# Values spread by DMAs, layer 3's heads on their own array rows, and probabilities turned in two row halves

## The chip, the cores and the metric

One core of a Trainium2 chip runs the whole program. The metric is the device time of that core in microseconds, from the first to the last instruction and what lies around them; less is better. TensorE is PE in the profile (PEld is its weight load), VectorE is DVE, ScalarE is ACT, GpSimd is POOL, SyncE is SP. A "q" behind the name means the engine's sequencer, which waits, counts and issues DMAs.

## The reference

Four Swin blocks follow one another on x of shape (16, 56, 56, 96), float32. Each one normalizes, shifts the image by 3, cuts it into windows of 7x7 = 49 tokens, attends inside each window with a learned bias and a mask, projects, adds, normalizes again and runs an MLP of 96, 384 and 96 channels. Layers 0 to 2 have 12 heads of 8 channels, layer 3 has 4 heads of 24.

```python
qkv = (xw @ qkv_w + qkv_b).reshape(B*nW, N, 3, NH, hd)
q, k, v = qkv[:, :, 0], qkv[:, :, 1], qkv[:, :, 2]
attn = einsum('wqhd,wkhd->whqk', q * hd**-0.5, k) + rel_bias
attn = softmax(attn + attn_mask)
o = einsum('whqk,wkhd->wqhd', attn, v).reshape(B*nW, N, C)
x = x + roll(window_reverse(o @ proj_w + proj_b))
m = gelu(ln(x) @ fc1_w + fc1_b)      # layer 3 normalizes m again here
x = x + (m @ fc2_w + fc2_b)
```

## The kernel before

The batch is cut into 4 groups of 4 images. A group's tokens (128 pairs of windows) stay in `x`, which has room for two groups, while all four layers run over them. A pair of windows has 98 tokens on 98 partitions (two windows of N = 49). Four pairs are a quad, so a stage, attention or MLP of one layer, has NQ = 32 quads. `quad_steps` (L232) calls a body for each quad: four quads in straight code, the rest two at a time in a loop, and two more at each end, where `on(d)` says whether quad i+d exists. Every engine runs the same schedule; the order on each engine is the order in which its body is written, and semaphores (`a_...`) join them. `wait(s, u)` (L260, its waits show as L262) stands until quad or pair u is counted on s. The order on each engine is strict: what stands behind a wait waits too.

The body of attention has four slots, s = 0 to 3, one for each pair of quad i. A pair goes through this chain:

- PE, L697: scores of pair s. Layers 0 to 2: three groups of 4 heads, each on 32 rows of the array (`QT` and `Kbd`, keys spread block-diagonally over a head slot and zeros), each into its own bank (0 to 2); layer 3: one group on all 96 rows. Windows 0 and 1 of the pair land on output partitions 0 to 48 and 64 to 112.
- DVE, L992 and L994: the bias is added while the scores are read from PSUM, then the maximum of each head is taken. POOL, L465, subtracts it. ACT, L555, takes the exponential in place, in `S`.
- PE, L753, in the next slot: one transpose per pair of heads turns 113 x 98 probabilities into 98 x 113 in PSUM (6 for 12 heads, 2 for 4 heads; banks 3 and 4). ACT, L579, copies them to `PT`.
- PE, L711, two slots later: `PT` times values, 2 per pair of heads, into bank 5 (`Ops`), with a column of ones that gives the sum. Both heads of a pair are contracted at once, so `Vbd` holds the values block-diagonally, with zeros where key and head don't match.

Around that, once per quad, PE also runs: in slot 0 the output projection of quad i-2 (L719, `Yps`, bank 6) and the first half of the values of quad i+1 (L675, 4 matmuls, bank 7); in slot 1 keys (L667, bank 6) and queries (bank 7) of quad i+1; in slot 2 the other half of the values (4 matmuls); in slot 3 the transposes of the outputs `Ot` (L738) and of the normalized tokens of quad i+2 (L745). For the values the tokens of each window stand twice in `hT`, so that the product has them on all 98 partitions, and DVE (L966) multiplies by the 0/1 mask `vmask` on the way into `Vbd`, twice a quad. DVE also adds the residual (L999, slot 0), takes statistics (L838 and L846, slot 1), and in slot 2 divides by the sums: `rec` at L1006, `Ot` at L1010. Since `Ops` is one bank, PE's product for the first pair of the next quad, which stands in slot 3, waits for `Ot`:

```python
if s == 3:
    wait(a_o, i - 1)
    wait(a_v0e, i)
```

ACT copies the keys four times, each with another `kmask` column (`key_slot`, L535), and the queries once (L560), all in slots 1 and 2. An fp32 matmul shows as two instructions in the profile, a transpose as one.

SP loads the constants (L343 to L371), then layer 0's mask, two DMAs a quad of 49 x 4 runs of 196 bytes (`mask_quad`, L302), each in turn when its place is free; and a group's tokens in 228 DMAs in and 228 out (`tokens`, L287). Stores of group g-1 and then loads of group g+1 are issued from the end of layer 0's attention of group g.

Of the kernel before, what the change touches and what calls it, by code (L numbers as in the profile page):

```python
# [30 lines left out]
TABLE = 2 * WS - 1  # L31
P = 128
# [48 lines left out]
def constants():  # L81
# [5 lines left out]
    c["kmask"] = np.stack([((ch // 8) % 4)[:, None] == np.arange(4)[None],  # L87
                           (ch // 24)[:, None] == np.arange(4)[None]], 1).astype(np.float32).reshape(C, 8)

    half = (np.arange(2 * N) // N)[:, None]  # L90
    c["vmask"] = np.concatenate([(half == (np.arange(w) // (w // 2))[None]) for w in (16, 48)],
                                1).astype(np.float32)
    c["vones"] = (half == np.arange(2)[None]).astype(np.float32)
# [16 lines left out]
def build(nc, d, x_in, out):  # L110
    ctx = ExitStack()
    with ctx:
# [3 lines left out]
        def sem(name):  # L116
# [17 lines left out]
        kmask = sb("kmask", [C, 2, 4])  # L134
        vmask = sb("vmask", [2 * N, 64])
        vones = sb("vones", [2 * N, 2])
        average = sb("average", [PAIR, PAIR])
        wqkv = sb("wqkv", [C + 1, LAYERS, 3 * C])
# [9 lines left out]
        hT = sb("hT", [C + 1, QUAD, 2, 2, N])  # L148
        QT = sb("QT", [C, 2, QUAD, PAIR])
# [3 lines left out]
        PT = sb("PT", [PAIR, 4, 6, 2, N])  # L153
        Vroom = sb("Vroom", [PAIR, 2 * QUAD * 2 * 108])
# [15 lines left out]
        Vbd = Vroom[:, :].rearrange("p (s j w t n) -> p s j w t n", s=2, j=QUAD, w=2, t=6)  # L170
        Vbd3 = Vroom[:, 0:2 * QUAD * 2 * 100].rearrange("p (s j w t n) -> p s j w t n", s=2, j=QUAD, w=2, t=2)
# [14 lines left out]
        a_xn, a_t1, a_ht, a_v0, a_v0e, a_k, a_ke, a_q, a_qe, a_v2, a_v2e = (sem(n) for n in (  # L186
            "xn_ready", "xnT_done", "hT_ready", "v_first_done", "v_first_ready", "k_done", "k_ready",
            "q_done", "q_ready", "v_second_done", "v_second_ready"))
# [6 lines left out]
        s_ones = sem("output_pads_set")  # L195
        s_stand = sem("waits_held")
# [23 lines left out]
        PTps = ps[0:PAIR, 3:5, 0:3 * P].rearrange("p b (g q) -> p b g q", q=ROW2)  # L220
        O_BANK, Z_BANK, X_BANK = 5, 6, 7
        XTps = ps[0:C, X_BANK, 0:QUAD * PAIR]
        Vps = ps[0:PAIR, X_BANK, 0:4 * C]
        Kps = ps[0:C, Z_BANK, 0:QUAD * PAIR]
# [7 lines left out]
        def quad_steps(eng, base, body, full=4):  # L232
# [13 lines left out]
            for i in range(NQ - skew, NQ + skew + 1):  # L246
                body(Unit(0, base, i, 0, pbase), i, lambda d: 0 <= i + d < NQ)

# [60 lines left out]
        def mask_stream(sp, g):  # L309
            with sp.Fori(2, NQ, 2) as q:  # L310
                for j in range(2):
                    sp.wait_ge(a_mb, g * NP + q * QUAD + (j - 1) * QUAD)
                    mask_quad(sp, g, q + j, j)

# [22 lines left out]
        def _(sp):  # L337
# [7 lines left out]
            load(kmask[:, :, :].rearrange("p a b -> p (a b)"), d["kmask"])  # L345
            load(vmask[:, :], d["vmask"])
            load(vones[:, :], d["vones"])
            load(average[:, :], d["average"])
            for l in range(LAYERS):
# [7 lines left out]
                load(wqkv[0:C, l, :], d[k["wqkv"]])  # L357
                load(wqkv[C:C + 1, l, :], row("bqkv"))
# [15 lines left out]
            mask_stream(sp, 0)  # L374
            with sp.Fori(1, GROUPS) as g:

                tokens(sp, g, False, s_x)
                sp.wait_ge(a_mb, g * NP)
                for q in range(2):
                    mask_quad(sp, g, q, q)  # L380
                sp.wait_ge(s_x, (g + 1) * (16 * LOADS))
                sp.sem_inc(s_next, 1)
                sp.wait_ge(s_fin, g)
                stand(sp)
                mask_stream(sp, g)
                tokens(sp, g - 1, True, s_out)
                sp.wait_ge(s_out, g * (16 * TOK_DMAS))
                stand(sp)
# [12 lines left out]
        def _(pool):  # L401

            for t in (mask0, room):
                pool.memset(t[:], 0.0)
# [710 lines left out]
```

## Time and profile before

| | |
|---|---|
| Time, median of 3 runs | 9466.97 us (9449.72 to 9478.86) |
| Time of the profiled execution | 9446.19 us |
| Its span | 9444.4 us |
| Mean granted TensorE clock | 0.970 |
| PE busy | 8794.8 us (93%), 110128 matmuls |
| PEld busy | 6584.9 us (70%) |
| DVE busy | 6697.5 us (71%) |
| ACT busy | 5517.5 us (58%) |
| POOL busy | 5081.6 us (54%) |

The first and last start of a score matmul (L697) bound each attention stage. For the second group they are 2503.9 and 2882.6 in layer 0, 3081.8 and 3473.0 in layer 1, 3662.0 and 4053.0 in layer 2, 4242.8 and 4516.5 in layer 3; between them lie the MLPs. A matmul's length includes its way through the array, and matmuls overlap, so the time that one costs is the step from one start to the next, not its length.

### The profile page before, as it was taken

Reading aid. Unit: us, or ns where it says so; the run is one execution under the profiler, and the core shown is the slowest. Engines: PE = TensorE matmul, PEld = TensorE weight load, DVE = VectorE, ACT = ScalarE, POOL = GpSimd, SP = SyncE. Lnnn points to the kernel's source line nnn. Section 1 sums busy time; section 2 is a strip of 40 time slices with the busy share of each in tenths; the row PEclk is TensorE's granted clock in tenths of the full one; section 3 lists DMA queues with packets and bytes.
Section 4 is the critical chain, followed back from the end, with each engine's and each line's share of the span. In section 5 each row is a group of like instructions: output and inputs, shape, how many; then the busy total and the mean of one; then the engine's idle time right before and its main releaser. Section 6 shows DMA issues by size and latency. Waiting matters only on the chain.

```text
span 9444.4 us, 315493 instructions
## 1 busy us (share of the span) xinstructions
PE 8794.8 (93%) x110128; PEld 6584.9 (70%) x110128; DVE 6697.5 (71%) x19998; ACT 5517.5 (58%) x9632; POOL 5081.6 (54%) x6190
## 2 busy tenths in 40 slices
PE   2999999998999999999899999999989999999986
PEld 1777777776677777777567677777657777777764
DVE  3777767667776676767877677776686767677676
ACT  1756647465574665746567375664656657465554
POOL 5865646553484554645258465554527756455441
PEclk8999999999999999999999999999999999999998
DMA  2010000000001000000000100000000000000000
GB/s 35 7 22 3 0 1 0 1 1 0 4 6 30 15 1 1 0 1 0 0 5 9 33 8 1 1 0 1 0 0 7 19 8 0 1 1 1 1 0 21
DMA packets 177967, 57.28 MB, mean 6 GB/s; under 512 B 176379, under 2 KB 177412, under 8 KB 177499
## 3 DMA queue, kind: packets, MB, share of 16 engines
q1 hardware_dynamic: 158592, 47.28, 2.7%
q10 hardware_dynamic: 14027, 3.47, 0.2%
q8 instruction: 242, 3.96, 0.2%
q0 software_dynamic: 4880, 0.71, 0.1%
q14 instruction: 226, 1.85, 0.1%
HBM read 31.71 MB, written 19.27 MB: 5 GB/s over the span
## 4 chain that ended last, share of the span: by engine, by line
PE 41%; issue 25%; POOL 13%; DVE 12%; DVEq 3%; POOLq 2%; ACT 1%; ACTq 1%; DMA 0%
PE ps L711 5%; PE ps L753 5%; PE ps L697 5%; PE ps L667 4%; PE ps L675 4%; PE ps L768 4%; PE ps L791 4%; POOL G L451 4%; POOL S L465 3%; PE ps L719 3%; DVE xn L945 3%; DVE bst L838 2%; DVE bst L1055 2%; POOL rstd L439 2%; PE ps L738 2%
## 5 line engine op out<-in xcount | busy, mean ns | idle before, releaser
L465 POOL TENSOR_TENSOR S<-S,mx 113x588 f32<-113x588 f32 (+1 forms) x2048 | 2062.3, 1007 | 1995.2 <-DVE mx L994 1973.4
L579 ACT ACTIVATE PT<-ps 98x588 f32<-98x588 f32 (+1 forms) x2048 | 1178.5, 575 | 998.4 <-PE ps L753 955.3
L992 DVE TENSOR_TENSOR S<-ps,bias 113x588 f32<-113x588 f32 (+1 forms) x1536 | 970.4, 632 | 921.6 <-PE ps L697 907.7
L711 PEld LDWEIGHTS ps<-Vroom,PT 98*49 98x49 f32 x40960 | 1174.8, 128 | 543.7 <-issue 513.2
L535 ACT ACTIVATE room<-ps,kmask 96x392 f32<-96x392 f32 x2048 | 1190.1, 583 | 447.7 <-PE ps L667 447.7
L994 DVE TENSOR_REDUCE mx<-S 113x12 f32<-113x588 f32 (+1 forms) x2048 | 1359.3, 664 | 70.4
L753 PE MATMUL ps<-ident,S 113*98 113x113 f32 x10240 | 1366.2, 265 | 23.2 <-ACT S L555 23.0
L711 PE MATMUL ps<-Vroom,PT 98*49 98x18 f32 (+1 forms) x40960 | 1330.8, 202 | 34.6 <-DVE Ot L1010 12.0
L555 ACT ACTIVATE S<-S 113x588 f32<-113x588 f32 (+1 forms) x2048 | 1239.2, 605 | 64.0 <-POOL S L465 62.3
L768 PEld LDWEIGHTS ps<-w,G 128*98 128x98 f32 x12288 | 1144.4, 168 | 112.8 <-issue 61.1
L753 PEld LDWEIGHTS ps<-ident,S 113*98 113x98 f32 x10240 | 1055.0, 129 | 233.1 <-issue 192.5
L697 PE MATMUL ps<-room,QT 32*64 32x196 f32 (+2 forms) x20480 | 1162.2, 350 | 1.5 <-issue 0.2
L768 PE MATMUL ps<-w,G 128*98 128x96 f32 x12288 | 1155.0, 251 | 0.0
L838 DVE BATCH_NORM_STATS2 bst<-x 98x6 f32 (+1 forms) x4224 | 880.9, 254 | 237.3 <-DMA G<-k_mask_dram 119.3
L675 PE MATMUL ps<-wqkv,hT 97*98 97x96 f32 x8192 | 925.1, 256 | 0.7 <-ACT hT L571 0.6
L503 POOL TENSOR_TENSOR x<-x,c 98x384 f32 x512 | 512.1, 1000 | 714.9 <-DVE xn L945 714.9
L439 POOL TENSOR_TENSOR rstd<-rstd,neghalf 98x4 f32 (+1 forms) x768 | 786.9, 1025 | 144.7 <-POOL rstd L436 144.7
L791 PE MATMUL ps<-h,w 97*128 97x392 f32 x2304 | 833.3, 498 | 13.4 <-ACT G L604 10.8
L675 PEld LDWEIGHTS ps<-wqkv,hT 97*98 97x98 f32 x8192 | 798.8, 168 | 45.0 <-issue 12.7
L667 PE MATMUL ps<-hT,wqkv 97*96 97x392 f32 x2048 | 815.1, 519 | 0.0
L604 ACT ACTIVATE G<-ps 128x1176 f32<-128x1176 f32 x384 | 441.7, 1150 | 534.2 <-PE ps L791 534.1
L451 POOL TENSOR_TENSOR G<-bias,mask 113x588 f32<-113x588 f32 x512 | 683.4, 1335 | 0.0
(80 smaller groups left out, 11710.3 us busy)
## 6 DMA issues: line engine op xcount, KB each, us to landing
mask<-L_conv_mask_matrix_dram SPq DMA_DIRECT2D x256, 37.5 KB
x<-x_dram SPq DMA_DIRECT2D x56, 84.0 KB
out_dram<-x SPq DMA_DIRECT2D x48, 84.0 KB
x<-x_dram SPq DMA_DIRECT2D x234, 10.5 KB
out_dram<-x SPq DMA_DIRECT2D x228, 10.5 KB
out_dram<-x SPq DMA_DIRECT2D x180, 18.4 KB
x<-x_dram SPq DMA_DIRECT2D x168, 18.4 KB
x<-x_dram SPq DMA_DIRECT2D x64, 48.0 KB
```

What stands on the lines that cost most here:

```text
L465: pool.tensor_tensor(v, v, m, ALU.subtract).then_inc(a_sub, 1)
L535: return act.activation(Kbd[:, o, :, :, a, :].rearrange("p j w n -> p (j w) n"), Kps.rearrange("p (g n) -> p g n", n=N), ACT.Copy, scale=k ...
L555: act.activation(S[:, e, 0:nh * N], S[:, e, 0:nh * N], ACT.Exp).then_inc(a_exp, 1)
L579: act.activation(PT[:, (s + 3) % 4, 0:blocks, :, :].rearrange("p (b t) w n -> p b (t w) n", b=banks), PTps[:, 0:banks, 0:2 * k, 0:N], ACT. ...
L667: return pe.matmul(dst.rearrange("p (g n) -> p g n", n=N), wqkv[:, l, col:col + C], at, start=True, stop=True)
L675: last = pe.matmul(Vps[:, at:at + C], twice, wqkv[:, l, 2 * C:3 * C], start=True, stop=True)
L697: last = pe.matmul(out, q, Kbd[rows, t, s, w, :, :].rearrange("p a n -> p (a n)"), start=True, stop=True)
L711: last = pe.matmul(Ops[ROW2 * w:ROW2 * w + N, p, b, :], PT[:, p, b, w, :], room_of[:, o if s < 3 else t, p, w, b, :], start=True, stop=True)
L753: last = pe.transpose(at.rearrange("p w q -> p (w q)")[:, 0:TOK], S[:, e, PAIR * b:PAIR * (b + 1)], ident[0:TOK, 0:TOK])
L768: last = pe.matmul(ps[0:PAIR, 6 + t, C * j:C * (j + 1)], G[:, t, c, PAIR * j:PAIR * (j + 1)], w2[:, l, c, :], start=(c == 0), stop=(c == H ...
L791: last = pe.matmul(ps[:, 2 + c, 0:QUAD * PAIR], w1[:, l, P * c:P * (c + 1)], h4[:, s, :, :].rearrange("p a q -> p (a q)"), start=True, sto ...
L994: dve.reduce_max(mx[:, e, 0:nh], S[:, e, 0:n].rearrange("p (h k) -> p h k", k=N), axis=AX.X).then_inc(a_mx, 1)
```

## The change

Four things change.

1. Values. The four matmuls per quad (L675 becomes one block in slot 2) take each pair's 98 tokens once; `hT` holds them once. The columns of the value weights are loaded in an order that puts even heads first, then odd heads. DVE copies the product once per quad into `Vd`, where each head is followed by a column that holds 1. Then SP issues four DMAs per quad, each of 49 partitions x 4 pairs x 54 floats (50 in layer 3), which put `Vd` into the block-diagonal `Vbd`, whose zeros are set once at the start. SP waits for the copy (`a_vd`) and for the products of the quad that used this half of `Vbd`; PE waits for the landing (`s_vb`) before the first product of a quad, behind its wait for `Ot`, and DVE waits for the landing of the previous quad before it overwrites `Vd`.
2. SP's program becomes the same `quad_steps` as the engines'. Mask loads stand behind the spread in each body of layer 0. A group's stores follow the attention of layer 0, the next group's loads that of layer 1.
3. Layer 3. Query and key weights are loaded with each head's 24 columns in a group of 32 (the rest zero), so each head has 32 rows of the array. Scores are 8 matmuls of 49 columns instead of 2 of 196, into banks 0 to 3; ACT copies the keys once (128 x 392, `Kfull`) instead of four times.
4. Turning. With 12 heads, each window's rows of `S` are turned apart: 12 transposes of 49 rows, window 0 into bank 3 and window 1 into bank 4, instead of 6 of 113 rows. Layer 3 keeps its two.

Orders change with it: the key projection moves from slot 1 to 0 (bank 7), the queries stay in slot 1 (bank 6), ACT's first key copy now stands ahead of the exponential in slot 1, its last one in slot 3, and the copy into `hT` behind that into `PT`. On PE a count on `s_stand` stands between the waits and the transposes.

```diff
-        Vroom = sb("Vroom", [PAIR, 2 * QUAD * 2 * 108])
+        Vd = sb("Vd", [PAIR, QUAD, 2, HALF])
+        Vbd = sb("Vbd", [PAIR, 2, QUAD, 2, 2, HALF])
...
+                    def spread(i, j, on):
+                        if on(1):
+                            wait(a_vd, i + 1)
+                            stand(sp)
+                            wait(a_pv, i - 1)
+                            stand(sp)
+                            par = (j + 1) % 2
+                            for w in range(2):
+                                for a in range(2):
+                                    sp.dma_start(Vbd[N * a:N * (a + 1), par, :, w, a, 0:width],
+                                                 Vd[N * w:N * (w + 1), :, a, 0:width]).then_inc(s_vb[par], 16)
...
+                    quad_steps(sp, base, spread, 4)
+                    if l == 0 and g > 0:
+                        sp.wait_ge(s_fin, g)
+                        tokens(sp, g - 1, True, s_out)
+                    if l == 1 and g + 1 < GROUPS:
+                        if g > 0:
+                            sp.wait_ge(s_out, g * (16 * TOK_DMAS))
+                        tokens(sp, g + 1, False, s_x)
...
+                            if s == 1 and on(1):
+                                wait(a_k, i + 1)
+                                if nh == 12:
+                                    key_slot(0)
+                                else:
+                                    act.activation(Kfull[:, o, :, :].rearrange("p j n -> p (j n)"), Kps,
+                                                   ACT.Copy).then_inc(a_ke, 1)
+                            if s == 3 and nh == 12 and on(1):
+                                key_slot(3).then_inc(a_ke, 1)
...
-                                for k in range(3 if nh == 12 else 1):
-                                    rows = slice(32 * k, 32 * (k + 1)) if nh == 12 else slice(0, C)
+                                for k in range(3 if nh == 12 else 4):
+                                    rows = slice(GRP * k, GRP * (k + 1))
...
                                 if s == 3:
                                     wait(a_o, i - 1)
-                                    wait(a_v0e, i)
-                                if s == 1:
-                                    wait(a_v2e, i - 1)
+                                    spread = (g * LAYER_QUADS + l * NQ + i.index - t + 2) * 32
+                                    pe.wait_ge(s_vb[t], spread if i.static else pe.snap(spread))
...
                             if s == 0 and on(1):
                                 wait(a_ht, i + 1)
-                                values(0).then_inc(a_v0, 1)
+                                project(Kps, 1).then_inc(a_k, 1)
                             if s == 1 and on(1):
                                 wait(a_res, i - 2)
-                                project(Kps, C, tokens_of).then_inc(a_k, 1)
-                                wait(a_v0e, i + 1)
-                                project(XTps, 0, tokens_of).then_inc(a_q, 1)
+                                project(Qps, 0).then_inc(a_q, 1)
                             if s == 2 and on(1):
                                 wait(a_qe, i + 1)
-                                values(2).then_inc(a_v2, 1)
+                                for p in range(QUAD):
+                                    last = pe.matmul(Vps[:, C * p:C * (p + 1)], hT[:, p, :, :].rearrange("p w n -> p (w n)"),
+                                                     wqkv[:, qkv_at(l, 2):qkv_at(l, 2) + C], start=True, stop=True)
+                                last.then_inc(a_v, 1)
...
                                 wait(a_exp, prior)
+                                stand(pe)
                                 for b in range(blocks):
-                                    at = PTps[:, b // 3, 2 * (b % 3):2 * (b % 3) + 2, :]
-                                    last = pe.transpose(at.rearrange("p w q -> p (w q)")[:, 0:TOK],
-                                                        S[:, e, PAIR * b:PAIR * (b + 1)], ident[0:TOK, 0:TOK])
+                                    at = slice(PAIR * b, PAIR * (b + 1))
+                                    if nh == 12:
+                                        for w in range(2):
+                                            q = slice(ROW2 * w, ROW2 * w + N)
+                                            last = pe.transpose(PTps[:, w, N * b:N * (b + 1)], S[q, e, at], ident[q, q])
+                                    else:
+                                        last = pe.transpose(ps[0:PAIR, 4, P * b:P * b + TOK], S[:, e, at], ident[0:TOK, 0:TOK])
...
-                            if s == 0 and on(1):
-                                wait(a_v0, i + 1)
-                                values(0).then_inc(a_v0e, 1)
...
                             if s == 2 and on(1):
-                                wait(a_v2, i + 1)
-                                values(2).then_inc(a_v2e, 1)
+                                wait(a_v, i + 1)
+                                if on(0):
+                                    spread = (g * LAYER_QUADS + l * NQ + i.index - j % 2 + 2) * 32
+                                    dve.wait_ge(s_vb[j % 2], spread if i.static else dve.snap(spread))
+                                made = Vps.rearrange("p (g t n) -> p g t n", g=2 * QUAD, n=dh)
+                                dve.tensor_copy(dense, made).then_inc(a_vd, 1)
```

## Rows read from the trace of the kernel before

**Rows 1.** Windows: us, busy us (instructions) per engine, granted clock, DMA share, GB/s; attention, layer 1.

```profile
5401.00:5780.00 379.00, 373.78 (x6367) 286.85 (x6372) 294.55 (x648) 273.12 (x468) 234.57 (x274) 1.00 0.04 8
```

**Rows 2.** Source L697, one attention stage of layer 1, then layer 3: durations ns, first/last start.

```profile
L697 PE MATMUL ps<-room,QT x1536: 323/362/585, 5401.0 to 5780.1; 32*64 32x196 f32 x128, 32*49 32x196 f32 x64
...
L697 PE MATMUL ps<-room,QT x512: 328/348/382, 6536.7 to 6810.3; 96*64 96x196 f32 x86, 96*49 96x196 f32 x85
```

**Rows 3.** Timeline of PE, one quad, layer 1: start, length, line, xcount [idle before <-releaser].

```profile
3300.92 1.58 PE L667 MATMUL ps<-hT,wqkv 97*96 97x392 f32 x4
3302.34 0.74 PE L753 MATMUL ps<-ident,S 113*98 113x113 f32 x6
3303.02 0.57 PE L697 MATMUL ps<-room,QT 32*64 32x196 f32 x12
...
3304.18 0.93 PE L675 MATMUL ps<-wqkv,hT 97*98 97x96 f32 x8
...
3305.67 0.57 PE L697 MATMUL ps<-room,QT 32*64 32x196 f32 x12
3306.31 0.73 PE L711 MATMUL ps<-Vroom,PT 98*49 98x18 f32 x24
...
3310.40 0.86 PE L675 MATMUL ps<-wqkv,hT 97*98 97x96 f32 x8
3311.09 0.74 PE L753 MATMUL ps<-ident,S 113*98 113x113 f32 x6
3311.77 0.57 PE L697 MATMUL ps<-room,QT 32*64 32x196 f32 x12
```

**Rows 4.** Lines by form, whole span: busy us, mean ns of one, then idle before.

```profile
L753 PE MATMUL ps<-ident,S 113*98 113x113 f32 x10240 | 1366.2, 265 | 23.2 <-ACT S L555 23.0
...
L711 PE MATMUL ps<-Vroom,PT 98*49 98x18 f32 x36864 | 1143.7, 201 | 31.4 <-DVE Ot L1010 9.2
```

**Rows 5.** Source L262 from 3305 us: PE's sequencer standing at a wait.

```profile
L262 PEldq EVENT_SEMAPHORE  x1: 1097/1097/1097, 3305.2 to 3305.2; - x1
```

**Rows 6.** Timeline of DVE in the same quad.

```profile
3300.43 0.77 DVE L992 TENSOR_TENSOR S<-ps,bias 113x588 f32<-113x588 f32 x1 [0.45 <-PE ps L697]
...
3303.68 0.77 DVE L992 TENSOR_TENSOR S<-ps,bias 113x588 f32<-113x588 f32 x1 [0.51 <-PE ps L697]
...
3305.65 0.56 DVE L1010 TENSOR_TENSOR Ot<-ps,rec 113x384 f32<-113x384 f32 x1
```

**Rows 7.** Timeline of ACT in the same quad.

```profile
3303.12 0.66 ACT L579 ACTIVATE PT<-ps 98x588 f32<-98x588 f32 x1
3303.68 0.57 ACT L535 ACTIVATE room<-ps,kmask 96x392 f32<-96x392 f32 x1
3304.15 0.69 ACT L555 ACTIVATE S<-S 113x588 f32<-113x588 f32 x1
```

**Rows 8.** Timeline of DVE, one quad of layer 3.

```profile
4401.70 0.36 DVE L992 TENSOR_TENSOR S<-ps,bias 113x196 f32<-113x196 f32 x1
...
4404.07 0.36 DVE L992 TENSOR_TENSOR S<-ps,bias 113x196 f32<-113x196 f32 x1 [0.31 <-PE ps L697]
...
4405.02 0.56 DVE L1010 TENSOR_TENSOR Ot<-ps,rec 113x384 f32<-113x384 f32 x1
```

**Rows 9.** Timeline of PE, the same quad of layer 3.

```profile
4405.68 0.39 PE L711 MATMUL ps<-Vroom,PT 98*49 98x50 f32 x8
4406.32 0.56 PE L738 MATMUL ps<-ident,Ot 113*96 113x113 f32 x4 [0.26 <-ACT room L535]
```

**Rows 10.** Windows: three microseconds with two mask loads.

```profile
251.00:254.00 3.00, 2.84 (x55) 2.31 (x54) 2.92 (x6) 2.56 (x5) 2.21 (x3) 1.00 0.14 26
```

**Rows 11.** Source L307, the same two mask loads on SP.

```profile
L307 SPq DMA_DIRECT2D mask<-L_conv_mask_matrix_dram x2: 281/281/281, 251.3 to 251.8; - x2
```

**Rows 12.** Source L300, the stores of one group on SP.

```profile
L300 SPq DMA_DIRECT2D out_dram<-x x228: 252/262/2351, 2860.0 to 3029.4; - x114
```

**Rows 13.** Source L339, constant loads on SP at the start.

```profile
L339 SPq DMA_DIRECT2D wqkv<-L_conv_qkv_w_dram x4: 404/426/583, 88.1 to 106.1; - x4
```

More of the change, by code:

```diff
@@ L31 @@
 TABLE = 2 * WS - 1
+HALF = 54
+GRP = 32
 P = 128
@@ L85, in constants @@
     ch = np.arange(C)
[L87 to L93, printed above, removed]
+    c["kmask"] = (((ch // 8) % 4)[:, None] == np.arange(4)[None]).astype(np.float32)
     c["average"] = np.full((PAIR, PAIR), 1.0 / (PAIR * PAIRS_IMG), np.float32)
@@ L247, in quad_steps, with qkv_at, values_of @@
                 body(Unit(0, base, i, 0, pbase), i, lambda d: 0 <= i + d < NQ)
+        def qkv_at(l, j):
+            wide = C if HEADS[l] == 12 else P
+            return l * 3 * C + j * wide
+        def values_of(t, nh, b):
+            width = C // nh + 1
+            return t[:, :, b * width:(b + 1) * width]
         def outputs_of(nh):
@@ L356, in col @@
                     return d[k[name]].rearrange("(n a) -> n a", a=1)
-                load(wqkv[0:C, l, :], d[k["wqkv"]])
-                load(wqkv[C:C + 1, l, :], row("bqkv"))
+                dh = C // HEADS[l]
+                for rows, src in ((slice(0, C), d[k["wqkv"]]), (slice(C, C + 1), row("bqkv"))):
+                    for j in range(2):
+                        dst, part = wqkv[rows, qkv_at(l, j):qkv_at(l, j + 1)], src[:, C * j:C * (j + 1)]
+                        if HEADS[l] == 4:
+                            dst = dst.rearrange("c (h n) -> c h n", n=GRP)[:, :, 0:dh]
+                            part = part.rearrange("c (h n) -> c h n", n=dh)
+                        load(dst, part)
+                    for a in range(2):
+                        at = qkv_at(l, 2) + a * (C // 2)
+                        load(wqkv[rows, at:at + C // 2].rearrange("c (t n) -> c t n", n=dh),
+                             src[:, 2 * C:3 * C].rearrange("c (t a n) -> c t a n", a=2, n=dh)[:, :, a, :])
                 load(wp[0:C, l, :], d[k["wp"]])
@@ L401, in _ @@
         def _(pool):
-            for t in (mask0, room):
+            for t in (mask0, room, Vbd):
                 pool.memset(t[:], 0.0)
@@ L664, in attend, with project @@
                         t, o = j % 2, (j + 1) % 2
-                        def project(dst, col, at):
-                            return pe.matmul(dst.rearrange("p (g n) -> p g n", n=N), wqkv[:, l, col:col + C], at,
-                                             start=True, stop=True)
-                        def values(first):
-                            for jj in range(2):
-                                for w in range(2):
-                                    twice = hT[:, first + jj, w, :, :].rearrange("p a n -> p (a n)")
-                                    at = (2 * jj + w) * C
-                                    last = pe.matmul(Vps[:, at:at + C], twice, wqkv[:, l, 2 * C:3 * C],
-                                                     start=True, stop=True)
-                            return last
-                        tokens_of = hT[:, :, :, 0, :].rearrange("p j w n -> p (j w) n")
+                        def project(dst, which):
+                            at = slice(qkv_at(l, which), qkv_at(l, which + 1))
+                            return pe.matmul(dst[0:at.stop - at.start, :], wqkv[:, at],
+                                             hT[:, :, :, :].rearrange("p j w n -> p (j w n)"), start=True, stop=True)
                         for s in range(QUAD):
```

168 lines of the change are left out of this document (79 added, 89 removed).

## The prediction

> **What bounds the kernel now.** I read the windows first. In an attention stage of 12 heads PE is busy 373.8 of 379 us, DVE 294.6, ACT 273.1, POOL 234.6 [rows 1]. So PE sets the pace there. Then the stages' lengths: 379.1 us from the first to the last start of a score matmul in layer 1, 273.6 in layer 3 [rows 2]. That is 31.75 quads of 11.94 us (the first two are shorter; the repeating one takes 12.00) and of 8.62 us. Twelve such stages and four of layer 3 make some 5,700 of the 9,444 us. The rest is MLPs and the start, where the change does nothing except at the start.
>
> Then the timeline of one quad, to see whether PE also waits. From the scores of slot 1 (end 3300.34, which is 0.09 us before DVE's bias at 3300.43) to the next such end (3311.77 + 0.57 = 3312.34) it takes 12.00 us [rows 3, 6]. PE is nearly without a gap, with one exception that decides this forecast: the products in slot 3 start at 3306.31, though their scores started at 3305.67 and the next group follows such scores after 0.49 (3305.67 + 0.49 = 3306.16). PE's sequencer had stood 1.10 us at one wait, until 3306.25 [rows 5], and DVE's `Ot` ended at 3305.65 + 0.56 = 3306.21 [rows 6]. So today PE waits 0.15 us a quad for `Ot`. A faster PE will wait longer.
>
> **The change on PE, 12 heads.** Values: 16 instructions a quad become 8. The block in slot 0 goes, 0.69 us (3311.09 - 3310.40) [rows 3]. The key projection takes its place there: half of the step of the four L667, 1.42 / 2 = 0.71, which slot 1 loses [rows 3].
>
> Turning: six transposes take 0.68 us to the scores behind them [rows 3]. One lasts 265 ns [rows 4] and all six 0.74, so they start (0.74 - 0.265) / 5 = 0.095 us apart, and 0.68 - 5 x 0.095 = 0.205 is the last one and 0.11 for the passage to another shape of work. The new form, with 49 rows and 49 columns, is not in the trace. Lower bound: the products, also small and in two halves (of columns) of the array: (0.73 - 0.20) / 11.5 = 0.046 us per two [rows 3, 4]; six times that and 0.11 make 0.39. Upper bound: twelve, each as long as a full one now, 12 x 0.095 + 0.2 = 1.35. I take the first, since both kinds go to two separate parts of the array, but with 0.055 for two (98 columns of weights each, not 49) and the passage counted twice, because the transposes now have another shape than keys, queries and values ahead of them: 6 x 0.055 + 0.22 = 0.55. That is 0.12 less than now per pair (0.67 or 0.68).
>
> This is where the Trainium skill speaks against the change: TensorEngine Tiling (Array Packing), Tiling Modes, Key Properties, says that a change of the tiling mode, other than a change of tile, drains the engine. The 0.11 us behind the six transposes agrees. By it each turning has a drain ahead as well; without one the slot would be 0.44 and not 0.55.
>
> First half of a quad, scores of slot 1 to the products of slot 3: PE now needs 5.97 - 0.15 = 5.82 us, and loses the keys (0.71) and two turnings' gain (0.24): 4.87. Second half: 12.00 - 5.97 = 6.03, less 0.24, plus 0.02 for keys instead of values: 5.81. PE alone would need 10.68.
>
> **But DVE has not got faster there.** Between the end of slot 1's scores and `Ot` it does bias and maximum of slot 1, statistics, bias and maximum of slot 2, reciprocal, `Ot`. From 3300.34 to 3306.21 it is 5.87 us, of which 0.51 is idle, waiting for slot 2's scores [rows 6]. With PE earlier that idle time goes: 5.36, and 0.10 to PE's first product (3306.21 to 3306.31). The change touches none of these instructions. What it takes from DVE is one of two value copies, which stands behind `Ot` or in slot 0, not on this way. And PE now computes the count for `s_vb` and waits once more, behind the wait for `Ot`: a register step and a wait, which I put at 0.15 us (between nothing, if done while it waits, and 0.3). So the first half takes 5.36 + 0.10 + 0.15 = 5.61, not 4.87: PE stands 0.74 us a quad. That is a wait in place of work.
>
> ACT: the half-size `hT` copy and 588 probabilities as before. But the first key copy now stands between the copy to `PT` and the exponential of slot 1: 0.56 (3303.12 to 3303.68), 0.47 (to 3304.15), 0.69 [rows 7] and 0.16 for two hand-overs make 1.88 us from the end of one turning to the start of the next, in which PE has scores 0.49, products 0.66, queries 0.71: 1.86. No slack is left there, so I add 0.1 us a quad (0 to 0.3). Layer 0 has its `xn` on ACT besides, in slot 0, with as little slack; it is in the same 0.1.
>
> New quad: 5.61 + 5.81 + 0.1 = 11.5 us against 12.0. With some 31 full quads in 12 stages: -0.5 x 372 = -186 us.
>
> **Layer 3.** Here too PE waits for `Ot`: DVE needs from 4401.70 - 0.09 = 4401.61 to 4405.02 + 0.56 = 4405.58, less 0.31 idle: 3.66 [rows 8], with 0.10 and 0.15 3.91; now 4405.68 - 4401.61 = 4.07 [rows 8, 9]. The second half is 8.62 - 4.07 = 4.55. It loses 0.26, in which the transposes of `Ot` wait for ACT's key copies [rows 9]; ACT makes one copy now instead of four. Scores of 49 columns in 8 places at once instead of 196 in two: at most the 0.38 between scores and products, at least nothing; I take 0.08 each, 0.16 in this half, by its nearest term, the columns. 3.91 + 4.55 - 0.26 - 0.16 = 8.04, so -0.58 x 128 = -74 us. PE alone would fall further, as it also sheds a value block.
>
> **The DMAs.** Two mask DMAs (392 runs of 196 bytes) take 0.14 x 3 us x 16 = 6.7 us of engine time [rows 10], 17 ns a run. and all of it lies inside those 3 us, issue included. Four spreading DMAs have 784 runs, a tenth longer: by that at most 6.6 us. SP issues one in 0.28, half a microsecond apart [rows 11], so the last goes out 2 us after `Vd` is ready, and with as much again for the way the spread has landed after 5 to 8 us. It is wanted a full quad later (DVE's next copy into `Vd`; PE's products in the next body's slot 3), over 10 us. I count nothing; if it took 12 the quad would become 12 and more. The Trainium skill, DMA: Bandwidth & Descriptors, section Why a DMA increments its semaphore by 16 and not by 1, has a DMA use the largest number of engines up to 16 that divides its slowest dimension, 7 for 49 partitions: an estimate of 784 x 18 / 7 = 2.0 us for the runs, against 0.9 on all 16. No row shows the engines one by one; the sum is the same by either.
>
> SP's other work: a group's 228 stores took from 2860.0 to 3029.4 [rows 12], and layer 1's scores began at 3081.8. In the new order they start at the same place and hold back the first spread of layer 1, which is wanted about 12 us before those scores: 40 us of slack. Loads take as long after layer 1. Nothing, too. Cost if the cover fails: the overhang, once per group.
>
> **Start.** SP loads the constants in single file, one `wqkv` load in 0.43 [rows 13], 0.47 with the step between. Six more per layer, less two masks: 22 x 0.47 = 10 us, some of them in short runs: +13 us (0 to 40), as PE and DVE wait for all constants.
>
> **Sum.** -186 - 74 + 13 = -247 on the profiled execution's 9446.2: 9199. It lies 20.8 under the median of the runs, 9466.97, so as a median 9220.
>
> **Rivals.** (a) DVE's chain does not hold: the extra wait is free, ACT has its slack, turning costs 0.44. Then the quad is 5.46 + 5.59 = 11.05 or, were PE alone the bound, 10.3: -0.95 to -1.7 a quad, -350 to -630, and layer 3 at 7.6 gives -130: 8,730 to 9,000. For it: PE is 99% busy now. Against: the 0.15 us wait that is already there, and no DVE instruction of the chain goes.
>
> (b) The halves don't overlap: twelve turnings at 0.055 or more, 0.88 a pair. First half then 4.87 + 0.66 = 5.53, still under DVE's 5.61; second 5.81 + 0.66; quad 12.2. +0.2 x 372 - 74 + 13 = +13: about 9,480, no change. For it: nothing in the trace has transposes in parts of the array. Against: six score groups run side by side (12 in 0.57 us, where one lasts 0.35) [rows 3].
>
> (c) Slower: each half-height transpose costs what a full one does (0.095, the upper bound, 1.35 a pair). It decides as soon as a turning takes over 0.88. PE's halves become 6.5 and 7.4, the quad 13.9: +1.9 x 372 - 60 = +650: 10,100. For it: the weights to load are as many per transpose as before, 98 columns, and there are twice as many transposes.
>
> (d) The spread lands late, through SP or the queue: only above 10 us; quads of 12.5 or more, 9,650. Against: the masks' 17 ns.
>
> **Chances.** Forecast's mechanism 60%, (a) 17%, (b) 9%, (c) 7%, (d) 4%, 3% for something else. (b) comes out within 0.3% in five of its nine, and to either side in two each. The forecast's own range, from turning 0.45 to 0.7, wait 0 to 0.3, ACT 0 to 0.3, start 0 to 40, is 9,080 to 9,350. For 8 in 10 it reaches into (a) and to (b): 8,960 to 9,420. A difference under 0.3% (28 us) can't be told from no change. Faster: 60 + 17 + 2 and 2 of the rest, 0.81; same 0.06; slower 7 + 4 + 2, 0.13.
>
> **What would show it.** PE's busy share in attention falls to about 93%, and its idle time stands before L711's successor with `Ot` as releaser, 0.7 us once a quad; a turning (12 transposes) takes 0.5 to 0.6 to the scores; layer 1's stage is 364 us and not 379, layer 3's 255; PE never waits for `Vbd`'s DMA; SP's stores end before layer 1. Wrong if a turning takes 0.9 and more, if PE waits for `s_vb`, or if the quad falls under 11.

## The result, and the profile after

| | before | after |
|---|---|---|
| Time, median | 9472.92 us (9449.72 to 9523.09) | 11631.91 us (11556.78 to 11708.68, 4 runs) |
| Profiled execution, span | 9444.4 | 11555.0 |
| Mean granted TensorE clock | 0.970 | 0.690 |

The changed kernel is slower: ratio 1.2271 (1.2148 to 1.2394). The forecast was 9220 us, range 8960 to 9420. The difference is larger than that of any rival.

The page of after, its span, busy times and the row of the granted clock:

```profile
span 11555.0 us, 337792 instructions
PE 10896.4 (94%) x121392; PEld 7714.5 (67%) x121392; DVE 6529.3 (57%) x19486; ACT 5126.7 (44%) x9248; POOL 5089.6 (44%) x6192
PEclk7567575599757658559965855856995585675899
```

And the same row of before:

```profile
PEclk8999999999999999999999999999999999999998
```

PE gained 2,100 us of busy time, while its clock stands at half in long stretches (5 in a digit is 1.2 GHz, 9 is 2.4 GHz). DVE, ACT and POOL do less work or as much as before, in a longer span. The windows of after say which stretches: one from an attention stage of 12 heads, in its repeating part, nearly the whole first stage, and one that lies wholly in layer 3's attention.

```profile
400.00:500.00 100.00, 100.00 (x1216) 69.74 (x1214) 52.15 (x117) 48.85 (x89) 54.81 (x49) 0.50 0.06 13
240.00:780.00 540.00, 540.00 (x6550) 377.71 (x6550) 273.82 (x591) 262.82 (x473) 296.71 (x267) 0.50 0.07 14
2500.00:2700.00 200.00, 186.89 (x3302) 140.74 (x3301) 138.44 (x494) 107.40 (x300) 122.05 (x222) 1.00 0.10 20
```

Against [rows 1] the clock has gone from 1.00 to 0.50, and PE never waits for another engine. The scores of layer 1 and of layer 3 in the third group, as in [rows 2]:

```profile
L731 PE MATMUL ps<-room,QT x1536: 324/529/583, 6639.6 to 7204.1; 32*64 32x196 f32 x190, 32*49 32x196 f32 x2
L731 PE MATMUL ps<-room,QT x2048: 198/228/254, 8145.0 to 8396.9; 32*49 32x49 f32 x95, 32*64 32x49 f32 x92
```

Layer 1 takes 564.5 us for 379.1, layer 3 takes 251.9 for 273.6. All twelve stages of 12 heads are alike (564.5 to 565.6 us); all four of layer 3 are at full clock. The twelve cost 6779.4 - 4594.8 = +2,185 us, layer 3 gives -87, the start +11 (first score at 219.7, before at 208.8). That is +2,109 of the 2,110.6 us between the spans.

The timeline of PE at the first stage's start shows the fall, and further on the quad that then repeats:

```profile
224.06 0.50 PE L789 MATMUL ps<-ident,S 49*98 49x49 f32 x12
224.49 0.57 PE L731 MATMUL ps<-room,QT 32*64 32x196 f32 x12
...
227.09 0.50 PE L789 MATMUL ps<-ident,S 49*98 49x49 f32 x12 [1.17 <-ACT S L597]
227.52 0.57 PE L731 MATMUL ps<-room,QT 32*64 32x196 f32 x12
...
229.52 0.74 PE L789 MATMUL ps<-ident,S 49*98 49x49 f32 x12
230.18 0.94 PE L731 MATMUL ps<-room,QT 32*64 32x196 f32 x12
...
402.43 0.94 PE L731 MATMUL ps<-room,QT 32*64 32x196 f32 x12
403.30 1.19 PE L743 MATMUL ps<-Vbd,PT 98*49 98x18 f32 x24
404.42 1.64 PE L762 MATMUL ps<-wqkv,hT 97*98 97x96 f32 x8
405.99 0.73 PE L789 MATMUL ps<-ident,S 49*98 49x49 f32 x12
406.66 0.93 PE L731 MATMUL ps<-room,QT 32*64 32x196 f32 x12
```

At full clock twelve half-height transposes cost 0.43 us up to the scores (224.06 to 224.49). Then PE waits 1.17 us for the exponential of the first pair, since the pipeline is still empty; some 2 us later everything is slower: turning 0.66, scores 0.87 to the products, products 1.12. The quad is 18.21 us, and the clock comes back only with the MLP behind the stage (802.6).

Layer 3 is at full clock; its timeline, as in [rows 9]:

```profile
2606.79 0.39 PE L743 MATMUL ps<-Vbd,PT 98*49 98x50 f32 x8 [0.50 <-DVE Ot L1036]
2607.15 0.56 PE L770 MATMUL ps<-ident,Ot 113*96 113x113 f32 x4
```

Here the expected picture is seen: a wait for `Ot` of 0.50 us, none before the transposes of `Ot`, a quad of 8.0 (7.97 to 8.07).

### The profile page after: what moved, and what is told of

The parts are those of the page before. It is cut to its first block, busy times and chain, and to the rows that moved or that the text cites. A ratio compares the mean times of both kernels' runs of the same rounds, so it can differ in the third digit from the quotient of the medians.

```text
span 11555.0 us, 337792 instructions
## 1 busy us (share of the span) xinstructions
PE 10896.4 (94%) x121392; PEld 7714.5 (67%) x121392; DVE 6529.3 (57%) x19486; ACT 5126.7 (44%) x9248; POOL 5089.6 (44%) x6192
## 4 chain that ended last, share of the span: by engine, by line
PE 72%; DVE 12%; issue 9%; DVEq 3%; POOL 2%; ACTq 1%; ACT 0%; POOLq 0%; DMA 0%
PE ps L743 15%; PE ps L731 12%; PE ps L707 10%; PE ps L789 9%; PE ps L750 6%; PE ps L762 5%; PE ps L770 4%; PE ps L805 3%; PE ps L828 3%; DVE bst L875 3%; PE ps L777 2%; DVE xn L982 2%; DVE bst L1084 2%; DVE agg L883 1%; DVEq L982 1%
## 5 line engine op out<-in xcount | busy, mean ns | idle before, releaser
L743 PEld LDWEIGHTS ps<-Vbd,PT 98*49 98x49 f32 x40960 | 1793.9, 190 | 943.4 <-issue 499.0
L614 ACT ACTIVATE PT<-ps 98x588 f32<-98x588 f32 x1536 | 1012.1, 659 | 2496.4 <-PE ps L789 2496.4
L743 PE MATMUL ps<-Vbd,PT 98*49 98x18 f32 (+1 forms) x40960 | 2028.8, 246 | 68.9 <-DVE Ot L1036 68.2
L731 PE MATMUL ps<-room,QT 32*49 32x196 f32 (+3 forms) x26624 | 1606.3, 446 | 1.2 <-DVE S L1022 0.7
L789 PEld LDWEIGHTS ps<-ident,S 49*98 49x98 f32 x18432 | 879.9, 187 | 1021.4 <-issue 1019.6
L707 PE MATMUL ps<-hT,wqkv 97*96 97x392 f32 (+1 forms) x2048 | 1398.5, 779 | 1.2 <-ACT hT L621 1.2
L789 PE MATMUL ps<-ident,S 49*98 49x49 f32 x18432 | 1125.5, 285 | 14.5 <-ACT S L597 14.1
L1022 DVE TENSOR_TENSOR S<-ps,G 113x588 f32<-113x588 f32 x512 | 394.7, 771 | 894.3 <-PE ps L731 893.0
L750 PE MATMUL ps<-wp,OT 97*98 97x96 f32 x4096 | 755.9, 357 | 9.3 <-ACT OT L607 9.3
L731 PEld LDWEIGHTS ps<-room,QT 32*64 32x64 f32 (+1 forms) x26624 | 591.7, 165 | 244.2 <-issue 104.2
```

The costliest lines, as they stand in the source:

```text
L707: return pe.matmul(dst[0:at.stop - at.start, :], wqkv[:, at], hT[:, :, :, :].rearrange("p j w n -> p (j w n)"), start=True, stop=True)
L731: last = pe.matmul(out, q, keys, start=True, stop=True)
L743: last = pe.matmul(Ops[ROW2 * w:ROW2 * w + N, p, b, :].rearrange("p (a n) -> p a n", a=2), PT[:, p, w, N * b:N * (b + 1)], v, start=True, ...
L750: last = pe.matmul(Yps[:, C * p:C * (p + 1)], OT[:, p, :], wp[:, l, :], start=True, stop=True)
L789: last = pe.transpose(PTps[:, w, N * b:N * (b + 1)], S[q, e, at], ident[q, q])
L1022: dve.tensor_tensor(dst, scores, b, ALU.add).then_inc(a_bi, 1)
```

## The experiments

Where only a median and a range stand, the executions of that kernel lie too far apart for a ratio. "A stage falls" means below that its clock goes to 1.2 GHz and is still there at its end.

### Which part of the change is it?

`e1_full_turn`: the changed kernel with full-height transposes for the 12 heads, as before the change. The copy into `PT` and the products follow the other layout; of the edit only the turning is shown.

```diff
-for w in range(2):
-    q = slice(ROW2 * w, ROW2 * w + N)
-    last = pe.transpose(PTps[:, w, N * b:N * (b + 1)], S[q, e, at], ident[q, q])
+out = PTps[:, b // 3, 2 * (b % 3):2 * (b % 3) + 2, :]
+last = pe.transpose(out.rearrange("p w q -> p (w q)")[:, 0:TOK], S[:, e, at], ident[0:TOK, 0:TOK])
```

> The changed kernel with the turning of 12 heads as before (six transposes of 113 rows), all else changed. Theory A, the row-half transposes are what leaves the granted clock at 0.5 in the attention of 12 heads: the clock is 1.0 there, a quad takes 11.6 to 11.8 us (5.61 + 6.05 + 0.1), the time is 9,250 to 9,330. Theory B, PE simply has too little to do (one value block less, a longer wait for Ot) whatever shape the turning has: the clock stays at 0.5, a quad takes about 18 us and the time is 11,500 to 12,000.

Measured: 9348.66 us (9196.28 to 9454.51), before 9495.99 beside it. In the profiled execution no stage of 12 heads falls. Four of them begin with 41 to 126 us at the lower clock and come back; the last stage of layer 3 falls as a whole (398.3 us). One of the seven executions of the kernel before that ran beside it took 10,892 us, with a mean clock of 0.741, where the other six took 9,410 to 9,555. It left no trace, so which of its stages fell isn't known; but it shows that the kernel with full-height transposes can lose the clock for long too. It is the only such one of the 37 executions of the kernel before in this case.

`e2_half_turn_only`: the kernel before with the half-height transposes and PE's count on `s_stand` ahead of them, and nothing else of the change (again only the turning is shown).

```diff
+for w in range(2):
+    q = slice(ROW2 * w, ROW2 * w + N)
+    last = pe.transpose(PTps12[:, w, N * b:N * (b + 1)], S[q, e, PAIR * b:PAIR * (b + 1)], ident[q, q])
```

> The kernel before with one edit, the twelve row-half transposes. Theory A: the clock falls to 0.5 in the attention of 12 heads, PE is busy all the time, a quad is the changed kernel's 18.2 us and 1.4 for the second value block at half clock, 19.6; the time is 12,200 to 12,500. Theory B: with all other work of before the clock stays at 1.0, a quad takes 11.1 to 11.5 us, the time is 9,150 to 9,300. In both, layer 3 stays at 8.6 us a quad at full clock.

Measured: 11497.88 us (11377.70 to 11618.05). Nine of the twelve stages fall (603 to 605 us, quad 19.53). The other three, in layer 0, hold: quad 11.48 and 362.3 us, where before has 12.0. Those that fall do so in their first quads. PE waits there twice, and the second wait is 0.78 us in layers 1 and 2, whose eight stages all fall, and 0.26 in layer 0, where three of four hold. Here it is in layer 1, and then in layer 0:

```profile
777.71 0.54 PE L752 MATMUL ps<-ident,xn 98*96 98x98 f32 x4 [0.78 <-POOL xn L490]
```

```profile
217.61 0.50 PE L763 MATMUL ps<-ident,S 49*98 49x49 f32 x12 [0.26 <-ACT S L558]
```

A window in a fallen stage, and the wait in each quad of a stage that holds:

```profile
1000.00:1100.00 100.00, 100.00 (x1166) 72.22 (x1164) 48.92 (x107) 45.70 (x78) 38.92 (x47) 0.50 0.00 0
```

```profile
410.81 0.73 PE L717 MATMUL ps<-Vroom,PT 98*49 98x18 f32 x24 [0.28 <-ACT PT L583]
```

So it is the turning in halves, with or without the spread values and the new order, that makes most or all stages of 12 heads fall, and the same edit saves half a microsecond a quad where the clock holds. The rest of the change makes none of them fall in e1's profile. It isn't wholly free of blame: the stretches at the lower clock at a stage's start are longer in e1 (41 to 126 us) than in before (27 to 34), and a stage of layer 3 fell, which happens in the profile of neither before nor e2.

### Is it the wait for `Ot`, or PE's work being too thin?

`e3_filler_in_wait`: the changed kernel with one matmul of 432 columns on the whole array (its result is overwritten by the scores) ahead of the scores of slot 3, behind which PE waits for `Ot`. `e4_filler_each_slot`: the same in every slot. `<w2>` stands for the MLP weights `w2`, written as rows of columns.

```diff
+if nh == 12 and s == 3:
+    pe.matmul(ps[:, 0, 0:432], ident[:, :], <w2>[:, 0:432], start=True, stop=True)
```

> The changed kernel with one more matmul a quad in layers 0 to 2 (128 rows, 128 columns of weights, 432 columns moving, 0.72 us at full clock, its output is overwritten), just ahead of the scores of slot 3, where PE would wait for Ot at full clock. If what is missing is little, the clock returns to 1.0, the filler hides in the wait, a quad takes 11.2 to 11.5 us and the time is 9,100 to 9,250. If not, the clock stays at 0.5, the filler costs 1.44 a quad, and the time is 12,100 to 12,300.

> As the run before, with the same filler ahead of the scores of every slot, 2.9 us a quad at full clock. If work that fills the whole array brings the clock back: 1.0, a quad of 13.2 to 13.8 us, 9,800 to 10,100. If the half-height transposes pull the clock down whatever stands beside them: 0.5, a quad of 24 us, 13,700 to 14,100.

Measured: e3 10255.91 us (10126.66 to 12416.83; three executions took up to 10,382, one 12,417). In its profile eight of twelve stages hold, with quads of 11.34 (360 us); four fall (620 us), in their first quad, at the wait that is there because the pipeline is empty:

```profile
787.72 0.54 PE L792 MATMUL ps<-ident,S 49*98 49x49 f32 x12 [1.17 <-ACT S L597]
789.93 0.94 PE L734 MATMUL ps<-room,QT 32*64 32x196 f32 x12
```

The eight that hold have the same wait there (1.17 us up to 1598.47 in the third stage), so it doesn't make a stage fall each time.

e4: 10074.48, ratio 1.0652 (1.0527 to 1.0778); all stages hold, but the quad is 14.1. So a stage can fall in its first quads even with e3's filler, which comes only behind that wait. Whether it can also fall at the wait in each later quad is tested next.

### The two places apart

`e5_start_filler`: the changed kernel with one more matmul of 512 columns ahead of the turning of each of a stage's first four pairs, four in all (`busy(4, 1)` is one, into bank 4), nothing later. `e6_start_and_wait_filler`: these and the filler of e3. `e7_full_turn_start`: e1 with them. `e8_before_start`: the kernel before with them.

```diff
+if i.static and i.index == (0 if s >= 2 else 1):
+    busy(4, 1)
```

> The changed kernel with four fillers (128x128 by 512 columns, 0.43 us each at full clock and two instructions, so 0.86) in each attention stage only at its start: ahead of the turnings of slots 2 and 3 of the first quad and 0 and 1 of the second, where PE stands idle for want of exponentials. Theory C: the clock falls in the thin first quad, and at half clock a stage stays there; past it, the changed quads hold the full clock. Then all stages run at 1.0, quads of 12 heads take 11.3 to 11.5 us, the time is 9,150 to 9,280. Theory D: the steady quads of the changed kernel can't hold it, whatever the start: the clock falls some quads later and the time stays at 11,500 to 11,700.

> The same start fillers, and the 432-column filler of every slot 3 that a run before had. Theory C: no stage falls, 9,150 to 9,250, about as without the second filler. Theory D: the start fillers do not matter when the slot-3 filler is there, 3 or 4 of 12 stages still run at half clock, 10,100 or more.

> All of the change but the row-half turning, with the start fillers. Theory C: no stage spends 40 to 130 us at half clock at its start any more, layer 3 does not fall either, quads of 11.45, 9,170 to 9,260 in every execution. If the start has no part in it, the time scatters between 9,190 and 9,460 as without them.

> The kernel before with the start fillers. Theory C: the stages that now begin with 10 to 27 us at half clock do not, 9,400 to 9,440. Otherwise 9,450 to 9,500, the fillers' own time at most 40 us more.

Measured (before beside them 9487.36 us); quads, clocks and stages are those of the profiled executions:

| | median us | ratio to before | 12-head quad, clock | fallen stages |
|---|---|---|---|---|
| e5 | 11270.63 | 1.1875 (1.1829 to 1.1921) | 11.03, then 18.21 | 12, after 32 to 66 us |
| e6 | 9136.04 | 0.9633 (0.9598 to 0.9668) | 11.34, 1.0 | 0 |
| e7 | 9180.63 | 0.9684 (0.9648 to 0.9721) | 11.48, 1.0 | 0 |
| e8 | 9430.46 | 0.9942 (0.9916 to 0.9968) | 12.0, 1.0 | 0 |

e5's timeline of PE shows quads at full clock and the fall at a wait for `Ot`:

```profile
1002.04 0.57 PE L731 MATMUL ps<-room,QT 32*64 32x196 f32 x12
1003.15 0.73 PE L743 MATMUL ps<-Vbd,PT 98*49 98x18 f32 x24 [0.54 <-DVE Ot L1038]
...
1008.21 0.57 PE L731 MATMUL ps<-room,QT 32*64 32x196 f32 x12
...
1014.17 0.73 PE L743 MATMUL ps<-Vbd,PT 98*49 98x18 f32 x24 [0.53 <-DVE Ot L1038]
...
1025.30 0.73 PE L743 MATMUL ps<-Vbd,PT 98*49 98x18 f32 x24 [0.64 <-DVE Ot L1038]
...
1028.93 1.19 PE L743 MATMUL ps<-Vbd,PT 98*49 98x18 f32 x24
```

e8 says what the start fillers alone do for the kernel before: 0.6%. What e7 gains beyond that is the change's without its turning in halves.

e7 has a wait too, in each quad, and holds in all sixteen stages. Its window and its waits, first two of layer 1, then two of layer 0:

```profile
900.00:1000.00 100.00, 96.90 (x1699) 72.77 (x1696) 76.36 (x170) 71.78 (x130) 65.51 (x77) 1.00 0.07 15
```

```profile
1005.68 0.73 PE L746 MATMUL ps<-Vbd,PT 98*49 98x18 f32 x24 [0.32 <-ACT PT L616]
1017.18 0.73 PE L746 MATMUL ps<-Vbd,PT 98*49 98x18 f32 x24 [0.36 <-ACT PT L616]
```

```profile
405.58 0.73 PE L746 MATMUL ps<-Vbd,PT 98*49 98x18 f32 x24 [0.54 <-DVE Ot L1040]
417.23 0.73 PE L746 MATMUL ps<-Vbd,PT 98*49 98x18 f32 x24 [0.47 <-DVE Ot L1040]
```

The wait of 0.54 us for `Ot` at 405.58 is as long as e5's, in the same place. In layer 0 PE waits 0.20 to 0.64 us in almost every quad, and no stage falls. What e5 has and e7 hasn't is the half-height turning.

### How much must stand in the wait, and must it stand there?

`e9_thin_filler`: e6 with a filler on 32 rows and 64 columns of weights, still 432 columns of data, so that it runs beside the scores. `e12_thin_filler_slot0`: the same matmul, but in slot 0, where PE waits for nothing. `e13_thin_filler_216`: e9 with 216 columns.

```diff
-pe.matmul(ps[:, 0, 0:432], ident[:, :], <w2>[:, 0:432], ...)
+pe.matmul(ps[0:64, 0, 0:432], ident[0:32, 0:64], <w2>[0:32, 0:432], ...)
```

> As the kernel with both kinds of filler, but the slot-3 filler has 32 rows and 64 columns of weights instead of 128 and 128; its 432 moving columns, and so its length, are the same. Theory E, what counts for the clock is how long PE stands idle: the thin filler fills the wait as well, all stages hold 1.0, 9,130 to 9,160. Theory F, what counts is how much of the array the work fills: the clock falls some quads into the stages of 12 heads as it did without a slot-3 filler, and the time is 11,300 to 11,800.

> The changed kernel with the fillers at the start of each stage and the thin filler (32 rows, 64 weight columns, 432 columns of data) in every quad, but ahead of slot 0's scores, where PE waits for nothing, and no longer of slot 3's, where it waits for Ot. Its output is the reference's. PE gets the same work in each quad as with the thin filler in the wait, and keeps the wait of about 0.5 us. Idle theory (the wait for Ot once a quad is what lets the clock fall): the stages of 12 heads fall to 0.5 after some quads, as with the start fillers alone, 11,250 to 11,700 us. Work theory (how much PE is given in each quad decides, wherever it stands): all stages stay at 1.0, quads of about 11.35 us, 9,120 to 9,200 us.

> The changed kernel with the fillers at the start of each stage, in all four layers, and the thin filler in slot 3 cut from 432 to 216 columns, so that it fills only part of the wait for Ot. Its output is the reference's. If what is left of the wait is short enough for the clock, all stages stay at 1.0 and the quad is 11.1 to 11.2 us: 9,040 to 9,080 us, level with the 432 columns or up to 30 us below. If the rest of the wait lets the clock fall in some stage, that stage costs some 180 to 250 us more, and the time is over 9,200 us.

e9: 9071.80 us (9071.16 and 9072.44), ratio 0.9579 (0.9501 to 0.9658), every stage at full clock, quad 11.16, the lowest median of the study. In layers 1 and 2 hardly anything is left of the wait (PE is 99.97% busy in 900 to 1000); in layer 0 it is 0.11 to 0.28 us. Its slot 3:

```profile
907.22 0.57 PE L723 MATMUL ps<-w,ident 32*64 32x432 f32 x1
907.23 0.56 PE L734 MATMUL ps<-room,QT 32*49 32x196 f32 x10
907.63 0.52 PE L723 MATMUL ps<-w,ident 32*64 32x432 f32 x1
907.99 0.49 PE L734 MATMUL ps<-room,QT 32*64 32x196 f32 x2
908.49 0.73 PE L746 MATMUL ps<-Vbd,PT 98*49 98x18 f32 x24
```

e12: 11577.91 us (11469.35 to 11686.48). All twelve stages fall, 34 to 105 us after their start, though PE gets the same instructions per quad as in e9. The wait is what differs:

```profile
1027.29 0.57 PE L734 MATMUL ps<-room,QT 32*64 32x196 f32 x12
1028.40 0.73 PE L746 MATMUL ps<-Vbd,PT 98*49 98x18 f32 x24 [0.54 <-DVE Ot L1041]
```

e13: 10688.74 us (10355.39 to 10833.21). All twelve stages fall again, most of them later, 67 to 311 us into the stage. What was left of the wait, up to the fall (1038.9):

```profile
1005.23 0.73 PE L746 MATMUL ps<-Vbd,PT 98*49 98x18 f32 x24 [0.37 <-DVE Ot L1041]
...
1016.36 0.73 PE L746 MATMUL ps<-Vbd,PT 98*49 98x18 f32 x24 [0.30 <-DVE Ot L1041]
...
1038.67 1.02 PE L746 MATMUL ps<-Vbd,PT 98*49 98x18 f32 x24 [0.31 <-DVE Ot L1041]
```

I had expected that either it holds or single stages fall; that all fall, and late, is new. `e10_filler_216` and `e11_filler_324` have full-array fillers of 216 and 324 columns in slot 3, and the start fillers in the stages of 12 heads alone.

> Full-array filler of 216 columns (half the length) in slot 3, start fillers only in the stages of 12 heads. If this dose is enough to hold the clock, a quad takes 11.05 to 11.2 us and the time is 9,040 to 9,090. If not, some or all stages fall to 0.5 some quads after their start, 9,500 to 11,400. Layer 3 holds 1.0 without start fillers, or falls in single stages (it did so once with full-height turning).

> The same with 324 columns. If the dose that is needed lies under it: 1.0 throughout, a quad of 11.15 to 11.3 us, 9,080 to 9,120. If it lies between 324 and 432: stages fall, 9,500 or more.

e10: 9349.84 us (9206.31 to 9494.28). e11: 9218.18 (9066.33 to 9365.11). In their profiles no stage of 12 heads falls (quads of 11.16 and 11.18). A full-array matmul of 216 columns takes longer in slot 3 than the thin one and leaves PE 98.98% busy in a window of 100 us in layer 1. In layer 0 of e10 a wait is left in nearly every quad, 0.25 to 0.42 us, and all four stages hold with half-height transposes:

```profile
410.22 0.73 PE L746 MATMUL ps<-Vbd,PT 98*49 98x18 f32 x24 [0.26 <-DVE Ot L1041]
421.59 0.73 PE L746 MATMUL ps<-Vbd,PT 98*49 98x18 f32 x24 [0.33 <-DVE Ot L1041]
```

What falls is layer 3, now without its start fillers: two stages in e10, one in e11, 398 us each for 250. The executions of both lie in steps of some 145 us, about what one such stage costs.

## Why the prediction was wrong, step by step

**The step that failed is the sum.** It multiplied durations read at granted clock 1.00 [rows 1, 3] by 372 quads, "-186 - 74 + 13", as if the clock were a constant. No term and no rival had it. With the turning in halves the stages fall in their first quads, behind a wait of 1.17 us that no term had, and at 1.2 GHz the quad takes 18.21 us, not 11.5. Had they come through, the longer wait for `Ot`, which the prediction itself forecast as "a wait in place of work", would have brought them down too (e5). In the twelve stages this is worth +2,185 instead of -186.

Before's profile had a warning that I didn't follow up. Its mean clock is 0.970, and layer 1's stage in [rows 2] is 379.1 us long while two of the second group, 3081.8 to 3473.0 and 3662.0 to 4053.0, take 391. The timeline and a window of before at the start of such a stage, layer 2 of the first group:

```profile
1352.08 0.79 PE L753 MATMUL ps<-ident,S 113*98 113x113 f32 x6 [0.44 <-ACT S L555]
...
1354.60 0.77 PE L745 MATMUL ps<-ident,xn 98*96 98x98 f32 x4 [0.58 <-POOL xn L487]
1355.17 1.34 PE L753 MATMUL ps<-ident,S 113*98 113x113 f32 x6
```

```profile
1356.00:1390.00 34.00, 33.84 (x394) 25.53 (x392) 17.06 (x33) 16.85 (x29) 11.62 (x12) 0.62 0.01 2
```

So before falls too, behind two waits of half a microsecond, at 1354.8, and rises again at 1382.1, with PE 99% busy and full-height transposes. After, in 240 to 780, PE is 100% busy at the same lower clock and never rises. Four of before's twelve stages begin so and take 391 to 394 us. A forecast would have had to ask what the change does to such a start.

**What carried, at full clock.**
- Turning: forecast 0.55 (0.39 to 1.35), measured 0.43. A drain ahead of it is not seen: 0.44 was the sum without one. The Trainium skill, TensorEngine Tiling (Array Packing), Tiling Modes, Key Properties, has a drain at each change of tiling mode; the row agrees with one passage a turning, not two.
- The halves do overlap, so (b) and (c) fall. e2 alone gives 11.48 for 12.0.
- DVE's chain sets the first half: e5's waits for `Ot` of 0.54 and 0.53 (forecast 0.7). From the end of slot 1's scores to the products in slot 3 it is 5.40 us, forecast 5.61. DVE's part took 5.25 for 5.36, and from the end of `Ot` to the products it is 0.15, for which the forecast had 0.10 and 0.15 for PE's count: the count cost 0.05 at most. The second half is 5.63 for 5.81. The 0.1 for ACT was not needed. Quad 11.03: what rival (a) has (11.05), since it priced these three as nothing; but the chain that the forecast named is the bound. With e2's 11.48 and 11.03, half of the saving is the turning's.
- Layer 3: 7.93 a quad over the stage (251.9 / 31.75) for 8.04, stage 251.9 for 255.
- Start: +11 for +13.
- The spread: SP issues one in 0.78, not in 0.28, four take 3.1 us a quad; PE never waits for `Vbd`. Rival (d) falls. SP's stores of the first group are issued from 3611.2 to 3730.2, before the second group's scores of layer 1 at 3808.7, as forecast.

```profile
L401 SPq DMA_DIRECT2D Vbd<-Vd x2048: 782/783/1792, 216.7 to 11223.4; - x187
```

- "PE's busy share falls to about 93%" was wrong in direction: it is 100% in the fallen stages, where PE waits for nobody. Before its stages fall, e5 has 96% (21.14 of 22 us in 990 to 1012). A busy share without its clock says little.

**What is shown of the cause.** The half-height turning is what makes the stages of 12 heads fall in these kernels: e1 and after, e7 and e5 differ in it alone, e2 and before in it and PE's count ahead of it, and without it none of these stages falls in a profile. It isn't the only way to lose the clock: stages of layer 3 fall without it (e1, e10, e11), and one execution of before took 10,892 us. Once the start is covered, the wait in each quad matters as well: e5 and e12 fall with waits of 0.53 us and more, e13 with 0.19 to 0.46 in layers 1 and 2, and e6 and e9 hold without one, or with at most 0.28, with the same transposes. With full-height transposes waits of up to 0.64 do no harm (e7). That in the later quads it is the wait and not the amount of work is shown by e9 against e12, where one matmul is only moved. e2 fits with it: its nine fallen stages fell in their first quads, and the three that came through them held, with half-height transposes and a wait of 0.28 a quad. Layer 0 of e10 held too, with 0.25 to 0.42. That overlaps e13's waits, so no bound can be drawn from the length of a wait; the kernels differ in more than the wait. The Trainium skill, TensorE: Matmul & The Clock Gate, A second HAM failure mode, knows a kernel whose small idle times between groups of matmuls make the clock swing between its two levels. That agrees with the falls here, from short waits; but in the changed kernel the clock does not swing back within a stage, with PE 100% busy for 540 us.

**What stays open.** Why the half-height transposes keep the clock down when PE is fully busy at 1.2 GHz: that they use 49 of 128 rows each is an argument, not a measurement, since no run had other transposes of that height. Whether the share of the array or the rest of the wait separates e10 from e13 is open too: both differ, and the waits overlap. Why the same stage with the same wait at its start falls in one group and holds in another (e3, e2's layer 0) no run shows.

## What to carry to other kernels

Work out what a change does to TensorE's clock as a term of the sum: a faster PE that then waits for another engine at a stage's start or in every round can lose the clock for a whole stage, which here makes 565 us of some 357 (e9). Read the clock row before the busy row, and explain each dip in the kernel before, short ones too. Where a small wait can't be removed, a matmul with no use in exactly that place can pay: 32 rows and 64 weight columns, beside other work, turned 1.1875 times the time before (e5) into 0.9579 (e9). Keeping the full-height turning gets most of that without a matmul in the wait (e7, 0.9684).

## What was not expected of the hardware

- Two lasting levels under the same program: in e3 the stage of layer 1, and that of layer 2, takes 360 us in two groups and 620 in the other two, by whether it fell in its first quads.
- A matmul that is moved by one slot changes the time from 9,072 to 11,578 us (e9, e12), though it computes nothing.
- The waits after which stages fell are short: up to 1.18 us at a stage's start, 0.2 to 0.9 us once in 11 us later on, beside half-height transposes. With the shorter ones it tends to come later (32 to 66 us into the stage in e5, 34 to 105 in e12, 67 to 311 in e13).
- At the lower clock not everything takes double: turning 0.66 for 0.43, products 1.12 for 0.66, a quad 18.21 for 11.03.
- Layer 3, whose two transposes are of full height, also falls as a whole now and then (four of twelve stages in e1, e10, e11: 398 us for 250), but in the profile of none of the kernels with start fillers in layer 3.
